# Landmark attention in images of 512 tokens, scores turned and split into high and low halves, and the clearing of the sorted rows issued in three parts

## What is computed

```python
qkv = (x @ w_qkv).reshape(Bb, Nn, 3, H, hd).transpose(2, 0, 3, 1, 4)
q, k, v = (qkv[0], qkv[1], qkv[2])
q = q / scale
k_lm = k.reshape(Bb, H, m, Nn // m, hd).mean(axis=-2)
q_lm = q.reshape(Bb, H, m, Nn // m, hd).mean(axis=-2)
kernel1 = softmax(einsum('bhnd,bhmd->bhnm', q, k_lm), axis=-1)
kernel2 = softmax(einsum('bhld,bhmd->bhlm', q_lm, k_lm), axis=-1)
kernel3 = softmax(einsum('bhmd,bhnd->bhmn', q_lm, k), axis=-1)
SV = kernel1 @ iterative_inv(kernel2) @ (kernel3 @ v)
out = SV.transpose(0, 2, 1, 3).reshape(Bb, Nn, C) @ w_proj
```

## Time and profile before

| | |
|---|---|
| time, median of 3 runs | 897.43 us (896.67 to 903.52) |
| the profiled execution's own time | 895.95 us |
| its span, first to last instruction | 894.7 us |
| granted TensorE clock, mean | 0.949 of 2.4 GHz |
| TensorE matmul busy | 744.4 us (83%) |
| VectorE, ScalarE, GpSimd busy | 559.3, 412.0, 426.5 us |

### The profile page before, as it was taken

How to read it: one execution, slowest core, us unless ns; L and a number is a source line. 1 busy time by engine, 2 the same in 40 slices (tenths; PEclk the granted TensorE clock), 3 DMA queues, 4 the chain that set the end, 5 groups by cost and what they waited for, 6 DMA issues and landing times.

```text
span 894.7 us, 19460 instructions
## 1 busy us (share of the span) xinstructions
PE 744.4 (83%) x6670; PEld 571.5 (64%) x6670; DVE 559.3 (63%) x1668; ACT 412.0 (46%) x1007; POOL 426.5 (48%) x437
## 2 busy tenths in 40 slices
PE   7889988889999998889899578886987886788840
PEld 6778755569977876768777355553666774555530
DVE  5984597668767759877775245452976672345434
ACT  3657655556345535555523155650454312365620
POOL 4755520006400015645675157776337772477770
PEclk9999999999999989999999899996999998899985
DMA  9999999930000037001111244434101111344416
GB/s 231 214 219 219 213 215 213 212 63 4 4 1 1 1 95 259 1 21 46 40 56 52 70 119 113 116 85 165 52 24 52 56 58 46 83 106 107 114 55 243
DMA packets 118529, 90.46 MB, mean 101 GB/s; under 512 B 12064, under 2 KB 109728, under 8 KB 118432
## 3 DMA queue, kind: packets, MB, share of 16 engines
q1 hardware_dynamic: 101760, 66.46, 33.0%
q0 software_dynamic: 9216, 19.68, 6.4%
q10 hardware_dynamic: 7456, 3.07, 1.7%
HBM read 31.76 MB, written 57.41 MB: 100 GB/s over the span
## 4 chain that ended last, share of the span: by engine, by line
PE 46%; DVE 17%; issue 11%; POOL 11%; ACT 5%; DMA 4%; SPq 3%; ACTq 3%; DVEq 0%; POOLq 0%
POOL sorted_rows L453 8%; PE banks L1864 5%; PE banks L914 5%; PE banks L1322 4%; PE banks L1877 3%; PE banks L1923 3%; SPq L711 3%; PE banks L402 2%; PE banks L403 2%; PE banks L404 2%; PE banks L176 2%; PE banks L921 2%; POOL expert_rows L729 2%; DVE hT L1235 2%; PE banks L1912 2%
## 5 line engine op out<-in xcount | busy, mean ns | idle before, releaser
L729 POOL DMA_INDIRECT expert_rows<-y,goal x160 | 153.2, 957 | 104.4 <-DVE y L852 59.0
L453 POOL DMA_INDIRECT sorted_rows<-rows_x,row_of x128 | 125.7, 982 | 67.2 <-issue 37.2
L1194 ACT ACTIVATE ys<-banks,wtab 128x128 f32<-128x128 f32 x256 | 73.1, 370 | 61.6 <-PE banks L1322 51.3
L914 PE MATMUL banks<-routed_w,t 128*64 x320 | 82.3, 400 | 10.7 <-issue 5.4
L402 PE MATMUL banks<-x_high,w_high 128*128 128x512 f32 x192 | 85.6, 446 | 0.4 <-POOL w_low L1073 0.4
L1322 PE MATMUL banks<-w,hT 128*128 128x128 f32 x512 | 73.8, 289 | 11.8 <-DVE hT L1235 11.4
L914 PE MATMUL banks<-routed_scratch,t 128*64 128x256 f32 x320 | 82.4, 401 | 0.0
L208 POOL TENSOR_TENSOR rstd<-rstd,mhalf 128x4 f32<-128x4 f32 x24 | 25.6, 1065 | 117.8 <-DVE rstd L202 117.6
L1322 PEld LDWEIGHTS banks<-w,hT 128*128 128x128 f32 x512 | 67.1, 199 | 21.3 <-DVE hT L1235 19.1
L1120 POOL TENSOR_TENSOR x<-ys,x 128x512 f32<-128x512 f32 x43 | 55.0, 1279 | 52.3 <-ACT ys L1194 52.0
L404 PE MATMUL banks<-x_high,w_low 128*128 128x512 f32 x192 | 76.8, 400 | 0.0
(11 more groups left out here) (313 smaller groups left out, 1799.9 us busy)
## 6 DMA issues: line engine op xcount, KB each, us to landing
sorted_rows<-zeros SPq DMA_DIRECT2D x32, 1120.0 KB, 17.3
tile<-sorted_rows SPq DMA_DIRECT2D x252, 35.0 KB, 2.0
routed_w<-in_ffn_w SPq DMA_DIRECT2D x8, 768.0 KB, 10.9
w<-in_ffn_w SPq DMA_DIRECT2D x20, 192.0 KB, 5.6
expert_rows<-y,goal POOLq DMA_INDIRECT x160
tile<-sorted_rows ACTq DMA_DIRECT2D x68, 35.0 KB
sorted_rows<-rows_x,row_of POOLq DMA_INDIRECT x128
xnT<-expert_rows SPq DMA_DIRECT2D x2, 1024.0 KB, 5.6
```

Of the source, the lines that this page charges most:

```text
L453: POOL.indirect_dma_start(sorted_rows, bass.IndirectOffsetOnAxis(self.row_of[:, g, i:i + 1], 0), rows_x[:, 4 * g + i // TOPK, :], None).th ...
L729: POOL.indirect_dma_start(expert_rows, bass.IndirectOffsetOnAxis(goal[:, 4 * q + i:4 * q + i + 1], 0), y[q % 6][:, i * P:(i + 1) * P], Non ...
L914: last = PE.matmul(pairs(q)[ROWS * h:ROWS * h + ROWS, i, :], t[q % 2][:, rows], weights(q, i, h, slice(0, 2 * P)), start=True, stop=True)
L1194: last = SCL.mul(ys[s % 2][:, j * P:(j + 1) * P], bank[4 + s % 2][:, j * P:(j + 1) * P], wtab[:, t, e:e + 1])
```

## The change

Stage 4 now works on images of 512 tokens instead of tiles of 128.

- q and the landmark keys are split into a high part (`float32r`) and the rest, by GpSimd. SyncE stacks them by DMA on 96 partitions: for each group of four heads (32 features) q high, q high, q low in `qS`, and key high, key low, key high, masked by head, in `KS` (made by GpSimd). One matmul over 96 rows then sums the three products of high and low.
- `scores1(i)`, for each half (8 heads) of each 128 tokens, gives the maxima only: VectorE writes them negated into `mrow`, TensorE turns them (`turn_maxima`), ScalarE copies them into rows 96 to 111 of `qS` (`rows_of_maxima`), and `KS` has ones for the head there.
- `scores_turned(b, i)`: scores of two heads for 512 tokens, landmarks on partitions, the maximum already subtracted by the sixteen added rows (112 rows, `float32r`). ScalarE's exponential goes straight to `E1T2`. The eight transposes of a tile, their copies and the subtraction are gone.
- `values1(b, c)`: the values `WV` and the ones `OS` are the weights, 32 columns wide at column group 0, 32, 64 or 96 of the array, and the exponentials are the moving side, in fp32. The 16 sums of each token end on few columns; `reciprocals` inverts 128 columns, `spread1` spreads them with `REP`, `divide1` multiplies. `output` and `residual` work on 512 tokens.
- `WV`, `OS`, `REP`, `R1` lie where `QB` was, so that GpSimd makes them (`late_constants`) after stage 2 and before its first `A_part`. `qT`, `yT`, `svT` and the halves lie in buffers of other layers.
- The clearing: 24 transfers as before, 4 behind the stacking, 4 when the landmark values are made.

The rest of `attn0` waits on signals with other names and does the same work. The diff, cut to its core (the removed functions stand above):

```diff
+EARLY = 24
+def clear_sorted_rows(chunks):
+    for c in chunks:
         SP.dma_start(sorted_rows[c * 16 * P:(c + 1) * 16 * P, :].rearrange("(p r) w -> p r w", r=16),
                      zeros[:, :].unsqueeze(1).broadcast_to([P, 16, ROW])).then_inc(*zeroed.inc)
...
+    GH, STACK = 32, 96
+    NG4, MAXROWS = P // GH, slice(STACK, STACK + H)
+    qS = sb("qS", [STACK + H, NG4, T], F32R, scope)
+    KS = [home[0:STACK + H, n * H * M:(n + 1) * H * M] for home in (x_high, x_low) for n in range(2)]
...
+    mrow = own("mrow", [P, 4, P])
...
+    E1T2 = [E3T, [flat[:, n * GW:(n + 1) * GW] for flat in (kT, v_sb[:, :, :].rearrange("p t d -> p (t d)")) for n in range(4)]]
...
+        for n in range(3):
+            PO(POOL.tensor_copy(hm4[GH * n:GH * n + GH, :], headmask[GH * n:GH * n + GH, 4 * n:4 * n + 4]))
+        POOL.memset(mrow[:, :, :], 0.0).then_inc(*attn0_const.inc)
...
+        POOL.wait_ge(*k2_mm(B))
+        POOL.wait_ge(*s3_mm(NI))
+        PO(POOL.memset(WV[:, :, :, :], 0.0))
+        PO(POOL.memset(OS[:, :, :], 0.0))
+        PO(POOL.memset(REP[:, :, :], 1.0))
+        for k in range(NK):
+            for h, r in enumerate(HALF):
+                for c in (2 * k + h, 2 * k + h + H):
+                    last = POOL.memset(OS[r, k, c:c + 1], 1.0)
+        PO(last)
+        PO(POOL.affine_select(out=REP[:, :, :], in_=REP[:, :, :], compare_op=ALU.is_ge, fill=0.0,
+                              base=0, pattern=[[8 * GH, 4], [1, P]], channel_multiplier=-8))
+        POOL.affine_select(out=REP[:, :, :], in_=REP[:, :, :], compare_op=ALU.is_ge, fill=0.0,
+                           base=7, pattern=[[-8 * GH, 4], [-1, P]], channel_multiplier=8).then_inc(*late_const.inc)
...
+    AHEAD = [((8, 9), (10, 11), (12, 13), (14, 15), (16, 17), (18, 19)), ((20, 21), (22, 23), (24,), (25,), (26,), (27,)),
+             ((28, 29), (30, 31), (), (), (), ()), ((),) * 6, ((),) * 6]
+    TURNED = [((1, 0), (1, 1), (2, 0)), ((2, 1), None, (3, 0)), ((3, 1), None, None), (None,) * 3, (None,) * 3]
...
+            POOL.wait_ge(*q_ready(b + 1))
+            PO(POOL.tensor_copy(x_high[:, cols], qT[:, cols]))
+            POOL.tensor_tensor(x_low[:, cols], qT[:, cols], x_high[:, cols], ALU.subtract).then_inc(*q_split.inc)
...
+        k4 = klm[:, :, :].rearrange("p (a b) m -> p a (b m)", a=2)
+        PO(POOL.tensor_copy(k_high.bitcast(F32R), k4))
+        POOL.tensor_tensor(k_low.bitcast(F32R), k4, k_high, ALU.subtract).then_inc(*k_split.inc)
+        POOL.wait_ge(*k_split(1))
+        POOL.wait_ge(*q_stacked(3 * NG4))
+        for b in range(B):
+            PO(POOL.tensor_copy(KS[b][MAXROWS, :].rearrange("p (h m) -> p h m", m=M),
+                                ident[MAXROWS, MAXROWS].unsqueeze(2).broadcast_to([H, H, M])))
+        POOL.wait_ge(*k_stacked(6 * NG4))
+        for b in range(B):
+            POOL.tensor_tensor(KS[b][0:STACK, :].rearrange("p (g j m) -> p g j m", g=NG4, m=M),
+                               KL[b].unsqueeze(2).broadcast_to([STACK, NG4, 4, M]),
+                               hm4[:, :].unsqueeze(1).unsqueeze(3).broadcast_to([STACK, NG4, 4, M]), ALU.mult).then_inc(*KS_ready.inc)
+        late_constants()
         for n in range(5):
...
+        SP.wait_ge(*q_split(B))
+        for n, part in enumerate((x_high, x_high, x_low)):
+            for g in range(NG4):
+                SP.dma_start(qS[GH * n:GH * n + GH, g, :].bitcast(F32), part[GH * g:GH * g + GH, :].bitcast(F32)).then_inc(*q_stacked.inc)
+        SP.wait_ge(*k_split(1))
...
+        for n, part in enumerate((k_high, k_low, k_high)):
+            for g in range(NG4):
+                for half in range(2):
+                    SP.dma_start(kl[GH * n:GH * n + GH, 2 * half:2 * half + 2, g, :],
+                                 part[GH * g:GH * g + GH, half, :].rearrange("p (b m) -> p b m", m=M)).then_inc(*k_stacked.inc)
+        clear_sorted_rows(range(EARLY, EARLY + 4))
+        SP.wait_ge(*W_mm(1))
+        clear_sorted_rows(range(EARLY + 4, NE))
...
+        def rows_of_maxima(b, half):
+            SCL.wait_ge(*mT_mm(2 * b + half + 1))
+            cols = slice(half * 2 * P, (half + 1) * 2 * P)
+            SCL.copy(qS[MAXROWS, :, b * S + cols.start:b * S + cols.stop],
+                     bank[7][MAXROWS, cols].unsqueeze(1).broadcast_to([H, NG4, 2 * P])).then_inc(*mT_ready.inc)
+        def exp1(b, i):
+            SCL.wait_ge(*sT_mm(NK * b + i + 1))
+            if b > 1:
+                SCL.wait_ge(*sv_mm(2 * (b - 2) + i // 4 + 1))
+            SCL.activation(E1T2[b % 2][PAIRS[i]], bank[3 + i % 2][:, :], ACT.Exp).then_inc(*e1_ready.inc)
...
+        def evict_values(b):
+            SCL.wait_ge(*sv_mm(2 * b + 2))
...
+            SCL.copy(svT[b % 2], bank[5][:, :]).then_inc(*values_out.inc)
+        rows_of_maxima(0, 0)
+        rows_of_maxima(0, 1)
+        for b in range(B):
+            for i in range(NK):
+                exp1(b, i)
+                if b and i == 1:
+                    evict_values(b - 1)
+                if i == 2 and b in (1, 2):
+                    rows_of_maxima(b + 1, 0)
+                if i == 4 and TURNED[b][0]:
+                    rows_of_maxima(*TURNED[b][0])
+                if i == 6 and TURNED[b][1]:
+                    rows_of_maxima(*TURNED[b][1])
+        evict_values(B - 1)
...
+        def maxima(i):
+            b, t, h = i // 8, i // 2 % 4, i % 2
             DVE.wait_ge(*s1_mm(i + 1))
...
+            if b:
+                DVE.wait_ge(*mT_mm(2 * (b - 1) + t // 2 + 1))
+            DVE.tensor_reduce(out=mrow[:, t, STACK + 8 * h:STACK + 8 * h + 8], in_=pv(bank[i % 2]), axis=AX, op=ALU.max,
+                              negate=True).then_inc(*m1_ready.inc)
...
+        def evict_w():
+            DVE.wait_ge(*late_const(1))
+            DVE.wait_ge(*W_mm(1))
+            w = bank[5][:, 0:B * NK * HD].rearrange("p (b k d) -> p b k d", b=B, d=HD)
             for h, r in enumerate(HALF):
...
+                for i in range(2):
+                    c = 16 * i + HD * h
+                    last = DVE.scalar_tensor_tensor(
+                        out=WV[r, :, i:NK:2, c:c + HD], in0=w[r, :, i:NK:2, :],
+                        scalar=0.25 ** 6, in1=rden[r, :, i:NK:2].unsqueeze(3).broadcast_to([64, B, 4, HD]), op0=ALU.mult, op1=ALU.mult)
...
+        def reciprocals(b):
+            DVE.wait_ge(*sv_mm(2 * b + 2))
+            DVE.reciprocal(R1[:, :], bank[2][:, 0:P]).then_inc(*total_ready.inc)
+        def divide1(b):
+            DVE.wait_ge(*rep_mm(b + 1))
+            DVE.wait_ge(*values_out(b + 1))
+            DVE.tensor_tensor(svT[b % 2], svT[b % 2], bank[6][:, :], ALU.mult).then_inc(*svT_ready.inc)
+        def residual(b):
+            xb = x[:, b * TB:(b + 1) * TB, :]
+            DVE.wait_ge(*pr_mm(b + 1))
+            DVE.tensor_tensor(xb, bank[2][:, :].rearrange("p (j d) -> p j d", d=D), xb, ALU.add).then_inc(*res_done.inc)
...
+        for i in range(2, 8):
+            maxima(i)
+        evict_w()
+        for b in range(B + 1):
+            for piece, halves in enumerate(AHEAD[b]):
+                for i in halves:
+                    maxima(i)
+                if b and piece == 0:
+                    reciprocals(b - 1)
+                if b and piece == 1:
+                    divide1(b - 1)
+                if b and piece == 3:
+                    residual(b - 1)
...
+        def scores1(i):
...
+            if i < 2:
+                PE.wait_ge(*turn(next_ready, 6, 0))
...
-                PE.wait_ge(*e1_in(i - 2))
...
+                PE.wait_ge(*m1_ready(i - 1))
+            if i % 8 == 0:
+                PE.wait_ge(*KS_ready(b + 1))
+            if i == 0:
+                PE.wait_ge(*q_stacked(3 * NG4))
+            rows = slice(b * S + t * P, b * S + (t + 1) * P)
+            for g in (2 * h, 2 * h + 1):
+                last = PE.matmul(bank[i % 2][:, (g % 2) * 4 * M:(g % 2 + 1) * 4 * M], qS[0:STACK, g, rows],
+                                 KS[b][0:STACK, 4 * M * g:4 * M * (g + 1)], start=True, stop=True)
+            last.then_inc(*s1_mm.inc)
...
+                    last = PE.matmul(bank[5][r, c:c + HD], K[b][r, k, :], A[b][r, k, M:TC], start=True, stop=True)
...
+        def turn_maxima(b, half):
+            PE.wait_ge(*m1_ready(8 * b + 4 * half + 4))
+            if b or half:
+                PE.wait_ge(*mT_ready(2 * b + half))
+            else:
+                PE.wait_ge(*turn(next_ready, 6, 3))
+            for t in (2 * half, 2 * half + 1):
+                last = PE.transpose(bank[7][:, t * P:(t + 1) * P], mrow[:, t, :], ident[:, :])
+            last.then_inc(*mT_mm.inc)
...
+        def scores_turned(b, i):
+            g = NK * b + i
+            k = PAIRS[i]
+            if i == 0:
+                PE.wait_ge(*mT_ready(2 * b + 2))
+            if g > 1:
+                PE.wait_ge(*e1_ready(g - 1))
+            PE.matmul(bank[3 + i % 2][:, :], KS[b][:, 2 * M * k:2 * M * (k + 1)], qS[:, k // 2, b * S:(b + 1) * S],
```

(134 more changed lines are left out.)

165 lines of the change are left out of this document (48 added, 117 removed).

## The result

The changed kernel takes 876.13 us (median of four runs, 873.27 to 880.06), the kernel before 897.93 beside it: a ratio of 0.976, 95% interval 0.973 to 0.979. Predicted were 874.5. Unaltered on another occasion (`changed_again`) it came to 0.977 (0.973 to 0.981). In the profile of `clears_alone` the attention still ends where it did, so the difference lies behind it, and of those four runs the times inside the attention count most.

What follows compares the result with a forecast made beforehand. TensorE's columns were taken to bound the last stage. Its end at 302.8 instead of 327.2 gave 24.4 us, less 1.0 clock and 0.5 GpSimd: 22.9, so 873.0 profiled, 874.5 median; range 866 to 887.

Steps and rivals of the forecast that it cites:

- Prices: Last stage: time per TensorE, VectorE and ScalarE call; TensorE's work for one image 10.3 us, against 18.6 before.
- rounds: Last stage, counted between ends of second `values1` calls: 11.3, 10.3 and 8.4 us, to 297.8.
- Image 0: First image of the last stage: VectorE's twelve maxima set the pace; second `values1` ends at 267.8.
- Rival (a): Last stage: matmuls of 96 and 112 rows count as different shapes, 5.7 us more, about 880; chance 0.15.
- Rival (c): Maxima scores: float32r with 256 columns runs at fp32's pace, 0.86 a call, some 888 to 891; chance 0.06.
- (d): `values1`: column groups don't overlap at 512 columns, or fp32 pairs serialise; up to 40 us, 914 or 909; chance 0.04.
- Rival (b): Before the inverse: stacked keys land late and it waits, one for one beyond 182.5; at 190, about 882; chance 0.08.
- the constants: GpSimd after stage 2: at most 9 us, not before 185.5, ended by 194.5, before the first `A_part` at 199.43.
- The clock: TensorE below full clock: 1.0 us allowed, for gaps and the last matmuls at the new end.
- The sum: Whole attention: last residual at 302.8, 24.4 us earlier; 22.9 left after allowances for clock and GpSimd.
- Behind the attention: Rest of the kernel: all that follows waits for the layer's last residual and moves with it.
- GpSimd's extra work: Stage 2, beside VectorE: 0.5 us allowed against the gain.

Runs made afterwards that it cites:

- clears_alone: The kernel before with only its 32 clears split as in the change (24 ahead, 4, 4): ratio 0.997 to the kernel before.
- values_twice: The changed kernel with the four 512-column matmuls of each values call run once more, into a spare bank: ratio 0.986 to the kernel before.
- balanced: The changed kernel with 64-column landmark matmuls, spare matmuls in TensorE's waits, and two maxima moved from image 0 to image 1: ratio 0.970.
- no_clears_first: The changed kernel with no clears ahead of the attention, 28 behind the key stack, 4 behind the landmark values: ratio 1.008.

## Why the prediction was right

Its sum holds term by term but for the clock. Small misses offset each other, and the closeness of the total is in part luck, as the last points here show.

- *Prices.* 256 columns in float32r: 0.12, price 0.125. A turned score 0.235, price 0.23. `values1` 1.87, price 2.12: there is one change of shape in it, not two (0.99 in `values_twice` with the change, 0.86 without), so eight calls were costed 2 us too high. Spread 1.10 to 1.17 and output 0.89 to 1.17 (1.67 at the very end, as the clock falls), price 0.89 each. Reciprocal 0.97, price 0.9. In all, rounds of 10.8, 9.9 and 8.7 where 11.3, 10.3 and 8.4 were forecast, and an end of 5.36 for 5.0.
- *Image 0.* The prediction had VectorE set it. At full clock TensorE is busy for 12.5 of its 13.0 us, and moving two maxima away only moved the time to image 1 (`balanced`): that step isn't borne out.
- *Rival (a)*, shape changes between 96 and 112 rows, is refuted: 0.47 and 0.48 side by side in the chain leave no room for 0.19.
- *Rival (c)* and *(d)* are refuted by the same chain. What they feared is dear where it is made to happen: fp32 for both kinds of score costs the stage 32 us, at 0.86 a maxima call as priced, and matmuls in one group take 3.4 us for 0.86. At four groups of 512 columns the gain is fourfold, and not the 3.2 that was estimated from the 2.38 times for three column tiles in the Trainium skill (TensorE: Matmul & The Clock Gate, Part 3).
- *Rival (b)* didn't come, by a smaller room than one would like: 17 us in this profile, 7 to 9 in five later ones. The keys landed by 171.45 (forecast 167; 178 to 180 in most later profiles), the constants took 6.0 (bound 9) and ended at 194.4 (194.5).
- *The clock* is the term that was mis-sized. The prediction put 1.0 us for it and looked for it at the end. It cost 4.8 us in the stage, almost all in the opening and image 0, which took 16.2 in place of 13.9 (13.0 at full clock), and 2.7 us in stage 2, where a stretch of half clock put the inverse's start at 199.2 for 196.6.
- *The sum.* Last residual at 308.15, forecast 302.8: +2.6 stage 2, +0.7 opening, +2.3 image 0, -0.9 two rounds, +0.7 the last image and end, 5.4 in all. Of that 1.5 had been allowed, so the gain in the profiled run is 19.0, not 22.9. The profiled run is the slowest of four; the medians are 21.8 apart, and so the forecast is 1.6 us off.
- *Behind the attention.* That all that follows moves with the residual holds only roughly. From the loads to the end it was 568.7 us before, 571.9 in the changed kernel's first profile, whose whole gain is therefore 15.9, and 565.0 to 570.8 in the eight later profiles made beside a kernel before near 898. A few us either way here are no merit of the sum.

Whether stage 2's half clock belongs to the change stays open. Up to it the instructions and gaps of TensorE are those of before (waits of 1.12 and 1.38 us at 126 and 134). Three profiles of the twelve with the new stage 2 have it, the two without that stage have none, which is no proof. In those three stage 2 takes 80.0 to 82.2 us. In the other nine it takes 77.3 to 77.5, where the kernel before has 77.3: the 0.5 us allowed for GpSimd's extra work wasn't spent.

## What to carry to other kernels

A change that makes TensorE's work shorter makes its waits count: price the clock with the same care as the columns, at the place where small matmuls and the first gaps meet, and fill both with columns that cost nothing. A step that waits in a queue behind bulk transfers has a threshold, and from there on loses one for one; work out the room on both sides of it, and look at more than one profile: here it was 17 us in the first and 7 in others. Bulk transfers moved "out of the way" should not lie beside a stage with thousands of short instructions.

## What the hardware did that was not expected

- TensorE's clock fell to 1.2 GHz with no idle time ahead of it. In the changed kernel it falls at 251.6, in the fourth batch of 32 matmuls of 64 x 8 (1.68 us in place of 1.10), and stays there through 11.5 us of image 0 in which TensorE is busy throughout:

```profile
249.89 1.10 PE L1979 MATMUL banks<-routed_w 64*64 64x8 f32 x32
...
251.36 1.68 PE L1979 MATMUL banks<-routed_w 64*64 64x8 f32 x32
```

```profile
257.20:268.70 11.50, 11.50 (x44) 9.03 (x48) 7.65 (x12) 6.57 (x10) 0.00 (x0) 0.50 1.19 220
```

  Nine profiles have these batches of 8 columns. In eight the clock falls within or between them; in `changed_again` all four batches take 1.10, and it falls right behind them. In all but `no_clears_first` TensorE had been busy throughout for 10 us and more before that. The three profiles with 64 columns there, at the same pace (1.10), have full clock through all four batches.
- Clears at 212 GB/s beside the inverse made it 18 us longer, in gaps behind every 128 matmuls or a multiple of it.
- Four column groups of fp32 matmuls with 512 columns: 0.86 us for what takes 3.4 one after another.
